# Cross-attention with layer norm: layer norm spread over two steps, scores of every fourth step from another buffer, and a context of ten 512-column matmuls ahead of them

## The chip, the cores and the metric

The kernel runs on one core of a Trainium2 chip. Its engines are TensorE (matmuls; PE in the profile, its weight loads PEld), VectorE (DVE), ScalarE (ACT), GpSimd (POOL) and SyncE (SP), which here only starts DMAs, in order. Engines meet through semaphores alone. The metric is the device time of one execution in microseconds; lower is better. Three runs before the change took 322.92 to 323.16 us, median 322.97.

## The reference

Eight batches of 256 queries (width 256) attend to 256 context rows (width 192), with eight heads of width 256. Then come the output projection, the residual and a layer norm. Cut to what matters:

```
Q = (x @ Wq)  K = (ctx @ Wk)  V = (ctx @ Wv)          # 8 heads of 256
score = einsum('bhqd,bhkd->bhqk', Q, K) / 16           # masked where mask == 0
attn  = softmax(score, axis=-1)
out   = concat_heads(attn @ V) @ Wo + x
out   = (out - mean(out)) * rsqrt(var(out) + 1e-5) * gamma + beta
```

## The kernel before, in words

The weights are folded once: A = Wk Wq per head, so that scores are ctx (A x), and C = Wv Wo per head, so that the output is the sum over heads of (attn ctx) C. Every float32 operand is split into a hi part (rounded, by ScalarE) and a lo part (the rest, by VectorE or GpSimd), and each product is the sum of three matmuls, hi hi, hi lo and lo hi.

The work is a chain of 32 steps t = 4b + j: eight batches b, four pairs of heads j = 0 to 3. In step t TensorE does, in this order (`step`, L527 to L538): the scores of t (20 matmuls of 256 columns), the query products g of t + 1 (18), the output products of t - 4 (18), and the context products of t - 3 (20). So the context products of pair j = 0 stand at the end of a step with j = 3, and the scores of j = 0 follow right behind them. Steps 0 to 5 are written out, steps 6 to 29 are a loop over b = 1 to 6 whose body is j = 2, 3, 0, 1, and the end is written out again.

The scores' stationary operand is g: gU (the upper 64 rows of both heads, hi and lo together), gL_hi and gL_lo. For t < 5 (`EARLY`) `g_tiles` (L118) hands out another buffer, `g_early`, for the same three tiles; the moving operand is always ctxT_hi or ctxT_lo. TensorE waits for gU (g_split, L402) before the first score matmul, and for gL_lo (L411) before the fifth.

The other engines follow in each step. VectorE takes scores and mask to negated scores and the row maxima, ScalarE does the exponentials, VectorE the inverse of the sums, GpSimd the normalising of probs, VectorE a transpose in squares of 32 x 32 for each head (L829). Between the two transposes VectorE writes the lo parts of g for the next step (`gU_lo_part`, `gL_lo_part`). SyncE carries the squares to memory and back as pT_raw (`carry_squares`, L283): one DMA out (L286), a wait until it has landed (L289), four DMAs in (L294). The next step's first transpose on VectorE writes the same squares tile, and so waits until that DMA has landed (L825).

The layer norm of batch b - 1 is done in the steps of batch b. VectorE adds the residual and takes the statistics at the end of j = 3 (of batch b), GpSimd makes rstd, and VectorE centres y (L885) and normalises it (L892) in j = 0 of the next batch. SyncE's loop body (L304 to L312) is, in its order: load xT, ctxT and mask of the next batch, carry the squares of j = 1, 2 and 3, load ctx and x, carry the squares of j = 0, and store the output (`store_out`, L236, which waits for the second normalised tile). Behind the store, the next pass of the loop begins with the three loads and the squares of j = 1.

`context_products` (L430) writes into a whole bank; its helper `halves` (L439) splits each product into two matmuls of 256 columns, one for each head, and only for t = 0 uses one of 512.

Of the kernel before, what the change touches and what calls it, by code (L numbers as in the profile page):

```python
# [25 lines left out]
PAIRS = H // 2  # L26
# [13 lines left out]
EARLY = 5  # L40

def attention_kernel(nc, xT, x, ctxT, ctx, mask, wqT, wkT, wvT, wo, gamma, beta, out, scratch):
    es = ExitStack()
    with es:
# [70 lines left out]

        y_last = probs[0][:, 0:QT, :]

        def g_tiles(t):  # L118

            if isinstance(t, int) and t < EARLY:  # L120
                return tuple(g_early[:, n] for n in range(3))
            return gL_hi[:], gL_lo[:], gU[:]

# [3 lines left out]
        gL_bank = bank("gL_bank", [P, 2, S])  # L127
# [196 lines left out]
        def _(pe):  # L324
# [65 lines left out]

            def scores(t, j, b, heads=(0, 1)):

                L_hi, L_lo, U = g_tiles(t)

                if j == 0:

                    pe.wait_ge(ctxT_split, b + 1)
                for hh in heads:
                    if hh == 0:

                        pe.wait_ge(g_hi_done, 3 * t + 3)
                        pe.wait_ge(g_split, 3 * t + 2)  # L402
                    for q in range(QT):
                        rows = slice(q * P, (q + 1) * P)
                        hi, lo, up = L_hi[:, hh, rows], L_lo[:, hh, rows], U[:, hh, rows]
# [24 lines left out]
            def context_products(t, j, b):  # L430

                if j == 0:

                    pe.wait_ge(C_split, 2 * (PAIRS - 1))

                    pe.wait_ge(ctx_split, 2 * b + 2)
                hi, lo, tL, tU = pT_hi[j % 2], pT_lo[j % 2], places("tL", t)[0], places("tU", t)[0]

                def halves(into, stationary, moving, first=False, last=False):  # L439

                    if isinstance(t, int) and t == 0:

                        return split_products(into[:], [(stationary, moving)], first=first, last=last)
                    for hh in range(2):
                        ins = split_products(into[:, hh, :], [(stationary, moving[:, hh, :])],
                                             first=first and hh == 0, last=last, shared=True)
                    return ins

                pe.wait_ge(pT_hi_done, 2 * t + 2)
                if isinstance(t, int) and t == STEPS - 1:  # L450

                    for k in range(KT):
                        halves(tU, ctxU[:, k, :], hi[:, k], first=k == 0)
                    pe.wait_ge(pT_split, 2 * t + 2)
                    for k in range(KT):
                        upper = halves(tU, ctxU[:, k, :], lo[:, k], last=k == KT - 1)
                    upper.then_inc(t_product, 1)
                    for k in range(KT):
                        halves(tL, ctxL_hi[:, k, :], hi[:, k], first=k == 0)
                        halves(tL, ctxL_lo[:, k, :], hi[:, k])  # L460
                        lower = halves(tL, ctxL_hi[:, k, :], lo[:, k], last=k == KT - 1)
                    lower.then_inc(t_product, 1)
                    return
                for k in range(KT):
                    halves(tL, ctxL_hi[:, k, :], hi[:, k], first=k == 0)
                    halves(tL, ctxL_lo[:, k, :], hi[:, k])

                if isinstance(t, int) and STEPS - 4 <= t < STEPS - 2:

                    pe.wait_ge(tU_summed, 2 * t)  # L470
                for k in range(KT):
                    halves(tU, ctxU[:, k, :], hi[:, k], first=k == 0)
                by_squares = not (isinstance(t, int) and t >= STEPS - 2)
                for k in range(KT):

                    pe.wait_ge(pT_split, 2 * t + (k + 1 if by_squares else 2))
                    end = k == KT - 1
                    lower = halves(tL, ctxL_hi[:, k, :], lo[:, k], last=end)
                    if end:
                        lower.then_inc(t_product, 1)  # L480
                    upper = halves(tU, ctxU[:, k, :], lo[:, k], last=end)
                upper.then_inc(t_product, 1)
# [99 lines left out]
        def _(act):  # L582
            def hi_part(dst, src):
                return nc.scalar.activation(dst, src, ACT.Copy)  # L584
# [21 lines left out]
                act.wait_ge(ctxT_in, 16 * b + 16)  # L606
                hi_part(ctxT_hi[:], ctxT_raw[:]).then_inc(ctxT_hi_done, 1)

            def gU_hi_part(t):

                act.wait_ge(g_product, 2 * t + 1)
                U = g_tiles(t)[2]
                hi_part(U[0:UP, 0, :], gU_bank[0:UP, 0, :]).then_inc(g_hi_done, 1)
                hi_part(U[UP:P, 1, :], gU_bank[UP:P, 0, :]).then_inc(g_hi_done, 1)

            def gL_hi_part(t):

                act.wait_ge(g_product, 2 * t + 2)
                hi_part(g_tiles(t)[0], gL_bank[:]).then_inc(g_hi_done, 1)

            def exponentials(t, j, heads=(0, 1)):
                if not (isinstance(t, int) and t < 2):
# [60 lines left out]
            def step(t, j, b, folds=()):  # L683
                before = not (isinstance(t, int) and t < OUT_LAG)
                if before:
                    t_hi_part(t - OUT_LAG)
                if j == PAIRS - 1 and not (isinstance(t, int) and t < PAIRS):
                    ctx_hi_part(b)
                exponentials(t, j, heads=[0])
                if before:  # L690
                    tU_hi_part(t - OUT_LAG)
                exponentials(t, j, heads=[1])
                if j == PAIRS - 1:
                    ctxT_hi_part(b + 1)
                gU_hi_part(t + 1)
                gL_hi_part(t + 1)
                if j == 2 and not (isinstance(b, int) and b == B - 1):
                    xT_hi_part(b + 1)
                if isinstance(t, int) and t == 1:
                    ctx_hi_part(b)  # L700
                if not (isinstance(t, int) and t < LAG - 1):
                    pT_hi_part(t - LAG + 1, (j - LAG + 1) % PAIRS)
                for pair in folds:
                    C_hi_part(pair)
# [6 lines left out]
            xT_hi_part(0)  # L711
            for h in range(2, H - 2):
                A_hi_part(h)
            gU_hi_part(0)
            gL_hi_part(0)
            ctxT_hi_part(0)
            for h in range(H - 2, H):
                A_hi_part(h)
# [29 lines left out]
        def _(dve):  # L748
# [33 lines left out]
                dve.wait_ge(mask_lowered, b + 1)  # L782
                nc.vector.tensor_scalar(mask_bias[:], mask_low[:], 4.0, None, ALU.mult).then_inc(mask_ready, 1)

            def gU_lo_part(t, hh):

                dve.wait_ge(g_hi_done, 3 * t + 1 + hh)
                own, other = (slice(0, UP), slice(UP, P))[::1 if hh == 0 else -1]
                U = g_tiles(t)[2]
                lo_part(U[other, hh, :], gU_bank[own, 0, :], U[own, hh, :]).then_inc(g_split, 1)  # L790

            def gL_lo_part(t):

                dve.wait_ge(g_hi_done, 3 * t + 3)
                L_hi, L_lo, _ = g_tiles(t)
                lo_part(L_lo, gL_bank[:], L_hi).then_inc(g_split, 1)

            def maxima(t, b, heads=(0, 1)):
# [97 lines left out]
            def centre(b):  # L896
                for q in range(QT):
                    if q == 0:

                        dve.wait_ge(mean_done, QT * b + QT)  # L900
                    centre_tile(y, q)
# [7 lines left out]
            def step(t, j, b, ends=None, folds=()):  # L909
# [16 lines left out]
                    finish_mask(b + 1)  # L926
                if by_squares:
                    transpose_squares(t, j, 0)
                if ends is not None and j == 0:
                    centre(ends)  # L930
                gU_lo_part(t + 1, 0)
                gU_lo_part(t + 1, 1)
                gL_lo_part(t + 1)
                if by_squares:
                    transpose_squares(t, j, 1)
                if ends is not None and j == 0:
                    normalise(ends)
                if ends is not None and j == 3:
                    add_residual(ends)
# [4 lines left out]
            dve.sem_inc(out_bank_read, 1)  # L944
            for h in range(H - 2):
                A_lo_part(h)
            gU_lo_part(0, 0)
            gU_lo_part(0, 1)
            gL_lo_part(0)
            for h in range(H - 2, H):  # L950
                A_lo_part(h)
            lower_mask(0)
# [7 lines left out]
            with dve.Fori(1, B - 1) as b:  # L960
                step(PAIRS * b + 2, 2, b)
                step(PAIRS * b + 3, 3, b, ends=b - 1)
                step(PAIRS * b + 4, 0, b + 1, ends=b - 1)
                step(PAIRS * b + 5, 1, b + 1)
            step(STEPS - 2, 2, B - 1)

            t_lo_part_lower(STEPS - 5)
# [186 lines left out]
```

## Time and profile before

| | |
|---|---|
| median of three runs | 322.97 us |
| the profiled execution | 323.15 us |
| its span, first to last instruction | 321.3 us |
| TensorE busy | 314.5 us (98%), 2574 matmuls |
| VectorE, ScalarE, GpSimd busy | 253.1 (79%), 221.9 (69%), 181.1 (56%) us |

The page gives the engines' busy time and 40 slices of the span. As TensorE's matmuls overlap, its pace is read from the starts in the timeline and not from the length of one (0.28 us). In a timeline a row is start, duration, engine, line, operation, output and inputs, count, and in brackets the idle time before it with its releaser.

### The profile page before, as it was taken

The numbers are of one execution on the slowest core, as the hardware profiler recorded it, in microseconds if no ns is written. First come the engines' busy times: TensorE is split into PE (matmuls) and PEld (weight loads), VectorE is DVE, ScalarE is ACT, GpSimd is POOL, SyncE is SP. The second block draws the span as 40 slices with busy tenths as digits, with TensorE's granted clock in tenths as the row PEclk, the third lists the DMA queues.
The fourth block names the chain that finished last, engine by engine and source line by source line (L and its number), as shares of the span: only waits on it lengthen the run. The fifth ranks groups of instructions, "written<-read, shape, count | busy, mean of one in ns | idle before, by whom it ended". The sixth has DMA issues, their size and how long they took to land.

```text
span 321.3 us, 8037 instructions
## 1 busy us (share of the span) xinstructions
PE 314.5 (98%) x2574; PEld 308.1 (96%) x2574; DVE 253.1 (79%) x721; ACT 221.9 (69%) x601; POOL 181.1 (56%) x183
## 2 busy tenths in 40 slices
PE   8999999999999999999999999999999999999993
PEld 7998888999999999999999999999999999999992
DVE  0466878778998889977997799977997799975686
ACT  2446677678777797668767787768766887767640
POOL 1122476558855586548755686457845686447311
PEclk9999999999999999999999999999999999999999
DMA  7995453453444545364356435354257435440001
GB/s 255 369 406 204 135 166 130 139 197 133 135 128 161 191 150 165 132 201 149 114 186 198 149 94 187 125 205 155 104 170 207 168 82 171 162 134 0 35 0 65
DMA packets 46911, 50.27 MB, mean 156 GB/s; under 512 B 3504, under 2 KB 37040, under 8 KB 46896
## 3 DMA queue, kind: packets, MB, share of 16 engines
q1 hardware_dynamic: 46608, 49.56, 46.1%
q10 hardware_dynamic: 288, 0.52, 0.7%
q8 instruction: 8, 0.13, 0.2%
q14 instruction: 7, 0.06, 0.1%
HBM read 32.24 MB, written 17.83 MB: 156 GB/s over the span
## 4 chain that ended last, share of the span: by engine, by line
PE 95%; DMA 2%; DVE 1%; SPq 1%; POOLq 0%; issue 0%; POOL 0%
PE score_bank L328 24%; PE out_bank L328 19%; PE gL_bank L328 14%; PE tL_bank L328 14%; PE tU_bank L328 9%; PE gU_bank L328 7%; DMA wq_raw<-in_wqT 2%; PE spare_bank L328 1%; PE spare_bank L362 1%; PE tL_bank L362 1%; PE tL_bank L344 1%; PE tU_bank L344 1%; PE out_bank L368 1%; PE tU_bank L368 1%; PE out_bank L344 0%; PE spare_bank L344 0%
## 5 line engine op out<-in xcount | busy, mean ns | idle before, releaser
L1033 POOL TENSOR_TENSOR probs<-probs,inv_sum 128x512 f32<-128x512 f32 x64 | 66.6, 1041 | 88.1 <-DVE inv_sum L819 87.5
L628 ACT ACTIVATE probs<-neg_scores,neg_max 128x256 f32<-128x256 f32 x128 | 64.2, 502 | 32.7 <-DVE neg_max L808 32.7
L1056 POOL TENSOR_TENSOR pT_lo<-pT_raw,pT_hi 128x512 fp32r<-128x512 f32 x60 | 76.5, 1295 | 8.6 <-ACT pT_hi L584 8.6
L808 DVE CUSTOM_DVE_ANT_0 neg_scores<-score_bank,mask_bias 128x256 f32<-128x256 f32 x128 | 49.2, 421 | 6.2 <-PE score_bank L328 3.7
L584 ACT ACTIVATE tL_hi<-tL_bank 128x512 fp32r<-128x512 f32 x31 | 18.6, 599 | 38.0 <-PE tL_bank L328 38.0
L829 DVE STREAM_TRANSPOSE squares<-probs 128x512 f32<-128x512 f32 x60 | 42.3, 706 | 0.6 <-DMA scratch<-squares 0.4
L754 DVE TENSOR_TENSOR tL_lo<-tL_bank,tL_hi 128x512 fp32r<-128x512 f32 x31 | 21.4, 689 | 22.7 <-ACT tL_hi L584 22.6
L328 PE MATMUL gL_bank<-xT_hi,A_hi 128*128 128x256 f32 x128 | 35.6, 278 | 0.0
L328 PE MATMUL gL_bank<-xT_lo,A_hi 128*128 128x256 f32 x128 | 35.6, 278 | 0.0
L328 PE MATMUL gL_bank<-xT_hi,A_lo 128*128 128x256 f32 x128 | 35.6, 278 | 0.0
L584 ACT ACTIVATE pT_hi<-pT_raw 128x512 fp32r<-128x512 f32 x60 | 34.3, 623 | 0.0
L328 PE MATMUL out_bank<-CL_lo,tL_hi 128*128 128x256 f32 x118 | 32.9, 279 | 0.0
L328 PE MATMUL out_bank<-CL_hi,tL_hi 128*128 128x256 f32 x118 | 32.9, 279 | 0.0
L328 PE MATMUL out_bank<-CL_hi,tL_lo 128*128 128x256 f32 x118 | 32.9, 279 | 0.0
L328 PE MATMUL score_bank<-ctxT_hi,gL_lo 128*128 128x256 f32 x108 | 30.1, 279 | 0.0
L328 PE MATMUL score_bank<-ctxT_hi,gL_hi 128*128 128x256 f32 x108 | 30.1, 279 | 0.0
L328 PE MATMUL score_bank<-ctxT_lo,gL_hi 128*128 128x256 f32 x108 | 30.1, 279 | 0.0
L328 PE MATMUL score_bank<-ctxT_hi,gU 128*128 128x256 f32 x108 | 30.1, 279 | 0.0
L328 PE MATMUL score_bank<-ctxT_lo,gU 128*128 128x256 f32 x108 | 30.1, 279 | 0.0
L856 DVE TENSOR_TENSOR tU<-tU_bank,tU_moved 64x256 f32<-64x256 f32 x62 | 26.0, 419 | 1.6 <-ACT tU_moved L669 0.6
L328 PE MATMUL tL_bank<-pT_hi,ctxL_hi 128*128 128x256 f32 (+1 forms) x122 | 24.6, 282 | 0.0
L328 PE MATMUL tL_bank<-pT_hi,ctxL_lo 128*128 128x256 f32 (+1 forms) x122 | 24.5, 281 | 0.0
(176 smaller groups left out, 1007.2 us busy)
## 6 DMA issues: line engine op xcount, KB each, us to landing
scratch<-squares SPq DMA_DIRECT2D x30, 512.0 KB, 2.6
pT_raw<-scratch SPq DMA_DIRECT2D x120, 128.0 KB, 3.1
xT_raw<-in_xT SPq DMA_DIRECT2D x8, 256.0 KB, 3.6
ctxT_raw<-in_ctxT SPq DMA_DIRECT2D x8, 256.0 KB, 3.8
wo_raw<-in_wo SPq DMA_DIRECT2D x4, 512.0 KB, 13.6
x_res<-in_x SPq DMA_DIRECT2D x8, 256.0 KB, 3.2
out<-y SPq DMA_DIRECT2D x7, 256.0 KB, 2.5
wq_raw<-in_wqT SPq DMA_DIRECT2D x3, 512.0 KB, 7.8
```

The lines of the kernel that those rows point to most:

```text
L328: ins = nc.tensor.matmul(into, stationary, moving, start=first and n == 0, stop=last and n == len(pairs) - 1, skip_group_check=shared)
L344: ins = nc.tensor.matmul(dst[:, i * DL:(i + 1) * DL], wq_raw[:, h * DT + d, i * P:(i + 1) * P], wk_raw[:, h * DT + d, :], start=d == 0, st ...
L362: ins = nc.tensor.matmul(lower[:, hh, :], wv_raw[:, h * DT + d, 0:P], wo_raw[:, h * DT + d, :], start=d == 0, stop=d == DT - 1)
L368: ins = nc.tensor.matmul(upper[hh * UP:(hh + 1) * UP, 0, :], wv_raw[:, h * DT + d, P:DL], wo_raw[:, h * DT + d, :], start=d == 0, stop=d = ...
L584: return nc.scalar.activation(dst, src, ACT.Copy)
L628: nc.scalar.activation(probs[j % 2][:, n, :], neg_scores[:, n, :], ACT.Exp, bias=neg_max[:, n:n + 1], scale=-1.0, accum_out=row_sum[:, n:n ...
L754: return nc.vector.tensor_tensor(dst, whole, hi.bitcast(F32), ALU.subtract)
L808: nc.vector.tensor_tensor_reduce(out=neg_scores[:, n, :], in0=score_bank[hh][:, q, :], in1=mask_bias[:], scale=-SCALE, scalar=3.0e38, op0= ...
L829: nc.vector.transpose(squares[:, :, rows, :].rearrange("p s n c -> p n s c"), probs[j % 2][:, rows, :].rearrange("p n (s c) -> p n s c", c ...
L856: nc.vector.tensor_tensor(tU[part, :], places("tU", t)[0][part, hh, :], tU_moved[part, :], ALU.add).then_inc(tU_summed, 1)
L1033: nc.gpsimd.tensor_tensor(probs[j % 2][:, rows, :], probs[j % 2][:, rows, :], inv, ALU.mult) \
L1056: nc.gpsimd.tensor_tensor(pT_lo[j % 2][:, k].rearrange("p hh (q i r) -> p (hh q) i r", q=QT, i=ROWS), pT_raw[j % 2][:, k].rearrange("p i n ...
```

## The change

Four edits. `g_tiles` gets j as well, and hands out `g_early` in every step with j = 0, not only for t < 5. `halves` uses one matmul of 512 columns whenever its pair is j = 0. On VectorE the centring of y stays in steps j = 0, but moves from ahead of the lo parts of g to behind the second transpose; the normalising moves from there to the same place of the step j = 1. SyncE's, GpSimd's and ScalarE's orders stay (ScalarE writes g_early instead of gU and gL_hi in these steps).

```diff
-        def g_tiles(t):
+        def g_tiles(t, j):
-            if isinstance(t, int) and t < EARLY:
+            if j == 0 or isinstance(t, int) and t < EARLY:
                 return tuple(g_early[:, n] for n in range(3))
...
                 def halves(into, stationary, moving, first=False, last=False):
-                    if isinstance(t, int) and t == 0:
+                    if j == 0:
                         return split_products(into[:], [(stationary, moving)], first=first, last=last)
...
-                if ends is not None and j == 0:
-                    centre(ends)
-                gU_lo_part(t + 1, 0)
-                gU_lo_part(t + 1, 1)
-                gL_lo_part(t + 1)
+                gU_lo_part(t + 1, (j + 1) % PAIRS, 0)
+                gU_lo_part(t + 1, (j + 1) % PAIRS, 1)
+                gL_lo_part(t + 1, (j + 1) % PAIRS)
                 if by_squares:
                     transpose_squares(t, j, 1)
                 if ends is not None and j == 0:
+                    centre(ends)
+                if ends is not None and j == 1:
                     normalise(ends)
...
-                step(PAIRS * b + 5, 1, b + 1)
+                step(PAIRS * b + 5, 1, b + 1, ends=b - 1)
```

What stands on TensorE before, in the loop, at the end of a step (context products into tL_bank and tU_bank, then the next scores):

```order
L449 ISA
L328 MATMUL tL_bank<-pT_hi,ctxL_hi 128x256 x2
L328 MATMUL tL_bank<-pT_hi,ctxL_lo 128x256 x2
L328 MATMUL tL_bank<-pT_hi,ctxL_hi 128x256 x2
L328 MATMUL tL_bank<-pT_hi,ctxL_lo 128x256 x2
L328 MATMUL tU_bank<-pT_hi,ctxU 128x256 x4
L476 REGISTER_ALU
L328 MATMUL tL_bank<-pT_lo,ctxL_hi 128x256 x2
```

And now, at the end of the loop's step j = 3 and the start of j = 0:

```order
L328 MATMUL tU_bank<-pT_hi,ctxU 128x512 x2
L476 REGISTER_ALU
L328 MATMUL tL_bank<-pT_lo,ctxL_hi 128x512
L328 MATMUL tU_bank<-pT_lo,ctxU 128x512
L328 MATMUL tL_bank<-pT_lo,ctxL_hi 128x512
L328 MATMUL tU_bank<-pT_lo,ctxU 128x512
L401 ISA
L402 REGISTER_ALU
L328 MATMUL score_bank<-ctxT_hi,g_early 128x256
L328 MATMUL score_bank<-ctxT_lo,g_early 128x256
```

The pairs of 256 columns have become single matmuls of 512, and the scores behind them read g_early; the count of columns is the same.

On VectorE, before, the end of the loop's step j = 0 (L885 centres, L754 are the lo parts of g and then of tL, L829 the transposes, L892 normalises):

```order
L829 STREAM_TRANSPOSE squares<-probs 128x2x8x32
L885 SCALAR_TENSOR_TENSOR y<-y,mean_var,gamma_sb 128x256 x2
L787 ISA
L754 TENSOR_TENSOR gU<-gU_bank,gU 64x256
L787 REGISTER_ALU
L754 TENSOR_TENSOR gU<-gU_bank,gU 64x256
L794 REGISTER_ALU
L754 TENSOR_TENSOR gL_lo<-gL_bank,gL_hi 128x512
L829 STREAM_TRANSPOSE squares<-probs 128x2x8x32
L892 SCALAR_TENSOR_TENSOR y<-y,rstd,beta_sb 128x256 x2
L845 ISA
L754 TENSOR_TENSOR tL_lo<-tL_bank,tL_hi 128x512
```

Now the same place:

```order
L829 STREAM_TRANSPOSE squares<-probs 128x2x8x32
L787 ISA
L754 TENSOR_TENSOR gU<-gU_bank,gU 64x256
L787 REGISTER_ALU
L754 TENSOR_TENSOR gU<-gU_bank,gU 64x256
L794 REGISTER_ALU
L754 TENSOR_TENSOR gL_lo<-gL_bank,gL_hi 128x512
L829 STREAM_TRANSPOSE squares<-probs 128x2x8x32
L885 SCALAR_TENSOR_TENSOR y<-y,mean_var,gamma_sb 128x256 x2
L845 ISA
L754 TENSOR_TENSOR tL_lo<-tL_bank,tL_hi 128x512
```

And the end of the loop's step j = 1, which before had nothing between its second transpose and the loop's branch:

```order
L754 TENSOR_TENSOR gL_lo<-gL_bank,gL_hi 128x512
L829 STREAM_TRANSPOSE squares<-probs 128x2x8x32
L892 SCALAR_TENSOR_TENSOR y<-y,rstd,beta_sb 128x256 x2
L960 REGISTER_ALU
L960 COMPARE_AND_BRANCH
```

The centring no longer stands ahead of gU and gL_lo, and the normalising is one step later.

## Rows read from the trace of the kernel before

**Rows 1.** The page: busy us (share) xinstructions; granted TensorE clock in 40 slices.
```profile
PE 314.5 (98%) x2574; PEld 308.1 (96%) x2574; DVE 253.1 (79%) x721; ACT 221.9 (69%) x601; POOL 181.1 (56%) x183
...
PEclk9999999999999999999999999999999999999999
```
**Rows 2.** Timeline of PE: first score matmuls of steps 6, 7, 14, 15.
```profile
68.70 0.28 PE L328 MATMUL score_bank<-ctxT_hi,gU 128*128 128x256 f32 x1
...
77.31 0.28 PE L328 MATMUL score_bank<-ctxT_hi,gU 128*128 128x256 f32 x1
...
139.31 0.28 PE L328 MATMUL score_bank<-ctxT_hi,gU 128*128 128x256 f32 x1
...
148.26 0.28 PE L328 MATMUL score_bank<-ctxT_hi,gU 128*128 128x256 f32 x1
```
**Rows 3.** Timeline of PE, step 9, fourth to sixth score matmul.
```profile
94.88 0.28 PE L328 MATMUL score_bank<-ctxT_lo,gL_hi 128*128 128x256 f32 x1
95.00 0.30 PE L328 MATMUL score_bank<-ctxT_hi,gL_lo 128*128 128x256 f32 x1
95.14 0.28 PE L328 MATMUL score_bank<-ctxT_hi,gU 128*128 128x256 f32 x1
```
**Rows 4.** Timeline of DVE, end of step 8.
```profile
92.08 1.15 DVE L885 SCALAR_TENSOR_TENSOR y<-y,mean_var,gamma_sb 128x256 f32<-128x256 f32 x2
...
94.17 0.69 DVE L754 TENSOR_TENSOR gL_lo<-gL_bank,gL_hi 128x512 fp32r<-128x512 f32 x1
94.78 0.71 DVE L829 STREAM_TRANSPOSE squares<-probs 128x512 f32<-128x512 f32 x1
95.40 0.95 DVE L892 SCALAR_TENSOR_TENSOR y<-y,rstd,beta_sb 128x256 f32<-128x256 f32 x2
```
**Rows 5.** Timeline of PE: query products ahead of the first g_early scores and behind them.
```profile
15.28 0.28 PE L328 MATMUL gL_bank<-xT_hi,A_hi 128*128 128x256 f32 x1
...
16.58 0.28 PE L328 MATMUL gL_bank<-xT_hi,A_lo 128*128 128x256 f32 x1
...
22.59 0.28 PE L328 MATMUL gL_bank<-xT_hi,A_hi 128*128 128x256 f32 x1
...
23.83 0.28 PE L328 MATMUL gL_bank<-xT_hi,A_lo 128*128 128x256 f32 x1
```
**Rows 6.** Timeline of PE: context of t = 0 in 512 columns, scores of step 4.
```profile
50.43 0.39 PE L328 MATMUL tL_bank<-pT_lo,ctxL_hi 128*128 128x512 f32 x1
...
51.35 0.28 PE L328 MATMUL score_bank<-ctxT_hi,g_early 128*128 128x256 f32 x1
...
53.74 0.28 PE L328 MATMUL gU_bank<-xT_hi,A_hi 128*128 128x256 f32 x1
```
**Rows 7.** Timeline of the SP queue (DMA issues), step 13.
```profile
136.08 0.37 SPq L239 DMA_DIRECT2D out<-y  x1
137.09 0.35 SPq L221 DMA_DIRECT2D xT_raw<-in_xT  x1
...
138.61 0.33 SPq L286 DMA_DIRECT2D scratch<-squares  x1
```
**Rows 8.** Line L286, the squares' DMA issued at 104.78, 138.61, 174.38.
```profile
DMA to landing us min/median/max: 4.2/4.2/4.2
...
DMA to landing us min/median/max: 4.9/4.9/4.9
...
DMA to landing us min/median/max: 4.1/4.1/4.1
```
**Rows 9.** Timeline of DVE: transposes of steps 5 and 10, gL_lo behind the latter.
```profile
67.42 0.70 DVE L829 STREAM_TRANSPOSE squares<-probs 128x512 f32<-128x512 f32 x1
...
109.04 0.71 DVE L829 STREAM_TRANSPOSE squares<-probs 128x512 f32<-128x512 f32 x1 [0.39 <-DMA scratch<-squares]
...
110.69 0.69 DVE L754 TENSOR_TENSOR gL_lo<-gL_bank,gL_hi 128x512 fp32r<-128x512 f32 x1
```
**Rows 10.** The page, DMA issues: count, KB, median us to landing.
```profile
scratch<-squares SPq DMA_DIRECT2D x30, 512.0 KB, 2.6
```

More of the change, by code:

```diff
@@ L391, in scores @@
             def scores(t, j, b, heads=(0, 1)):
-                L_hi, L_lo, U = g_tiles(t)
+                L_hi, L_lo, U = g_tiles(t, j)
                 if j == 0:
@@ L607, in ctxT_hi_part, with gU_hi_part, gL_hi_part @@
                 hi_part(ctxT_hi[:], ctxT_raw[:]).then_inc(ctxT_hi_done, 1)
-            def gU_hi_part(t):
+            def gU_hi_part(t, j):
                 act.wait_ge(g_product, 2 * t + 1)
-                U = g_tiles(t)[2]
+                U = g_tiles(t, j)[2]
                 hi_part(U[0:UP, 0, :], gU_bank[0:UP, 0, :]).then_inc(g_hi_done, 1)
                 hi_part(U[UP:P, 1, :], gU_bank[UP:P, 0, :]).then_inc(g_hi_done, 1)
-            def gL_hi_part(t):
+            def gL_hi_part(t, j):
                 act.wait_ge(g_product, 2 * t + 2)
-                hi_part(g_tiles(t)[0], gL_bank[:]).then_inc(g_hi_done, 1)
+                hi_part(g_tiles(t, j)[0], gL_bank[:]).then_inc(g_hi_done, 1)
             def exponentials(t, j, heads=(0, 1)):
@@ L694, in step @@
                     ctxT_hi_part(b + 1)
-                gU_hi_part(t + 1)
-                gL_hi_part(t + 1)
+                gU_hi_part(t + 1, (j + 1) % PAIRS)
+                gL_hi_part(t + 1, (j + 1) % PAIRS)
                 if j == 2 and not (isinstance(b, int) and b == B - 1):
@@ L713, in _ @@
                 A_hi_part(h)
-            gU_hi_part(0)
-            gL_hi_part(0)
+            gU_hi_part(0, 0)
+            gL_hi_part(0, 0)
             ctxT_hi_part(0)
@@ L783, in finish_mask, with gU_lo_part, gL_lo_part @@
                 nc.vector.tensor_scalar(mask_bias[:], mask_low[:], 4.0, None, ALU.mult).then_inc(mask_ready, 1)
-            def gU_lo_part(t, hh):
+            def gU_lo_part(t, j, hh):
                 dve.wait_ge(g_hi_done, 3 * t + 1 + hh)
                 own, other = (slice(0, UP), slice(UP, P))[::1 if hh == 0 else -1]
-                U = g_tiles(t)[2]
+                U = g_tiles(t, j)[2]
                 lo_part(U[other, hh, :], gU_bank[own, 0, :], U[own, hh, :]).then_inc(g_split, 1)
-            def gL_lo_part(t):
+            def gL_lo_part(t, j):
                 dve.wait_ge(g_hi_done, 3 * t + 3)
-                L_hi, L_lo, _ = g_tiles(t)
+                L_hi, L_lo, _ = g_tiles(t, j)
                 lo_part(L_lo, gL_bank[:], L_hi).then_inc(g_split, 1)
@@ L946, in _ @@
                 A_lo_part(h)
-            gU_lo_part(0, 0)
-            gU_lo_part(0, 1)
-            gL_lo_part(0)
+            gU_lo_part(0, 0, 0)
+            gU_lo_part(0, 0, 1)
+            gL_lo_part(0, 0)
             for h in range(H - 2, H):
```

## The prediction

> **What bounds the kernel now.** I read the page's busy shares first, then the timeline of TensorE, then those of VectorE and of the SyncE queue around one batch boundary, and last the landings of the squares DMA. TensorE is busy for 314.5 of 321.3 us at a granted clock of full speed in every slice [rows 1], so 2.4 GHz throughout, and nothing is missing to fill: only fewer or faster matmuls, or a new wait, can move the end.
>
> The reader should look at the starts. A step has 76 matmuls of 256 columns (20 scores, 18 query products, 18 output, 20 context). Step 6 runs from 68.70 to 77.31, 8.61 us or 113.3 ns each; step 14 runs from 139.31 to 148.26, 8.95 us or 117.8 ns each [rows 2]. The instructions are the same, the clock is the same and TensorE shows no gap in either. So there are two paces, 4.5 ns apart, and each lasts until something disturbs it. All steps to 8 have the fast one; from step 9 to the last steps all have the slow one.
>
> The change of pace has a place. In step 9 the fifth score matmul, the first to read gL_lo, starts at 95.00 and its successor at 95.14 instead of 0.113 later [rows 3]. gL_lo of this step was written by VectorE from 94.17 for 0.69, to 94.86, and ahead of it and gU stands the centring of y, 1.15 us from 92.08 [rows 4]. Without the centring gL_lo would be there at 93.71. A wait of a few hundredths was enough, and the fast pace did not come back by itself.
>
> What brings it back? Query product 0 ran 11 intervals from 15.28 to 16.58, 118 ns each, slow. Then came the first scores with g_early. The query products behind them ran 11 intervals from 22.59 to 23.83, 113 ns each, fast [rows 5]. Step 4 is the only place that has what all steps j = 0 have after the change: a context in 512 columns, 0.92 us for four matmuls (230 ns), then 20 scores with g_early in 2.39 us (51.35 to 53.74, 119.5 ns each) [rows 6], and behind it the fast pace again.
>
> **The change part by part.** Write S(t) for the start of step t's scores.
>
> Scores with g_early at t = 8, 12, ... 28: six times 20 matmuls at 119.5 ns instead of 117.8 (at t = 8 instead of 113.3). +0.03 each, +0.12 at t = 8.
>
> Context in 512 columns at the end of t = 11, 15, ... 27 (and 7, 31): ten at 230 ns against twenty at 117.8: 2.30 against 2.36, -0.05 each; against twenty at 113.3 (2.27) +0.03.
> The Trainium skill has a price here ("TensorE: Matmul & The Clock Gate", section Back-to-back issue gap): columns over 2.4 GHz plus about 2.5 ns for a matmul by itself, so 215.8 ns for 512 columns. This trace shows 230 [rows 6]; by the page's figure ten would take 2.16 us and each context would give another 0.14 us, an estimate.
>
> Pace, if it comes back at every j = 0: the steps j = 0, 1, 2 run fast. j = 0 takes 2.39 + 56 x 0.1133 = 8.73 us instead of 8.95 (-0.22), j = 1 and 2 take 8.61 (-0.34 each).
>
> The centring moves behind gL_lo and behind the second transpose of the squares. Per batch VectorE does as much as before. In step 8 gL_lo is ready at 93.71, 1.1 us before it is asked for, so step 9 is not disturbed: t = 9 and 10 gain 0.34 each. The squares of j = 0 steps are there 1.15 us earlier too.
>
> The normalising moves from the end of j = 0 to the end of j = 1. Here a queue pays that the diff does not touch. SyncE waits for y_out_done before it stores the output, and behind that store stand, in its one queue, the loads of xT, ctxT and mask and the squares of the same step j = 1. Before, the store of batch 1 was issued at 136.08 and the squares at 138.61, 2.53 us later, all without a wait [rows 7]. Now the store waits for the end of the normalising. In an undisturbed step the second transpose starts at 67.42 [rows 9]; the normalising starts 0.62 later, as from 94.78 to 95.40, and takes 0.95 [rows 4], so it ends at 68.99, S(6) + 0.29. The squares' DMA then goes out at S + 0.29 + 2.53 = S + 2.82 of the next step (j = 2), where it stood at S(14) - 0.70. Behind those loads it landed 4.2, 4.9, 4.1, 4.1 and 4.9 us later (steps 9, 13, 17, 21, 25; rows 8 show the first three) [rows 8], so at S + 6.9 to 7.7, and at 4.2 at S + 7.02.
>
> Who waits for it: VectorE's first transpose of step j = 2 (in step 10 it would have started at 109.04 - 0.39 = 108.65), and behind it gU, gL_lo and so TensorE's next scores. In step 10 this wait already shows: transpose at 109.04, 0.39 idle, gL_lo finished at 110.69 + 0.69 = 111.38, 2.34 after the transpose's start [rows 9]. With 0.06 from landing to transpose and 0.14 from gL_lo to its matmul [rows 3, 4], the fifth score matmul of the step j = 3 can start at S + 7.02 + 2.54 = S + 9.56. At the fast pace it is due at S + 8.61 + 0.45 = S + 9.06. So TensorE waits 0.50 us (0.40 at a landing of 4.1, 1.20 at 4.9). It happens after steps 10, 14, 18, 22 and 26; after the last store no loads follow, and step 30 transposes on TensorE. I take 4.2, the median of the five landings. That wait also costs the fast pace, as it did in step 9, so j = 3 stays at 117.8 ns until the next g_early scores.
>
> Sum against the profiled run's own span of 321.3: t = 8, +0.12; t = 9 and 10, -0.68; five groups of four steps (11 to 14, ..., 27 to 30), each -0.05 - 0.22 - 0.34 - 0.34 = -0.95, together -4.75; five waits of 0.50, +2.50; t = 31 and what follows to the transposes on TensorE, 58 matmuls x 4.5 ns, -0.26. Together -3.07. The profiled run took 323.15; the median of the runs, 322.97, is 0.18 below it. Forecast: 322.97 - 3.0 = 320.0 us, with own ends of 319.4 (all landings 4.1) and 323.4 (all landings 4.9).
>
> **Rivals.**
> 1. No wait at all. If the squares land 3.7 us or less after their issue (2.6 is the median of all 30 [rows 10]), gL_lo is in time, nothing disturbs the fast pace, and j = 3 gains too (56 x 0.1133 + 2.30 = 8.65, -0.30 instead of -0.05). Sum: 0.12 - 0.68 - 5 x 1.20 - 0.25 = -6.8, so 316.2 us. For it: the four reads of pT before the store are now over by the time of the loads. Against it: step 10 before, where the landing behind the three loads decided.
> 2. The pace does not come back in the loop. All five examples of g_early scores stand in code that runs once, and none was entered from the slow pace of 256-column matmuls. Then t = 9 and 10 gain 0.68, t = 8 costs 0.12, and the first wait makes the rest slow. At the slow pace the normalising ends at S + 0.1 and the wait is 0 to 0.7 a batch; with two of five landings at 4.9, +1.4. Sum +0.8, so 323.8 us. The page just named, same section, knows a gap that depends on columns alone and no lasting pace; by it the near weights would change nothing and this is the outcome. The two step lengths [rows 2] speak against the page: equal work, 0.34 us apart.
> 3. Slower through the queue. The pace comes back, but the loads and the squares, bunched behind the late store, land later than they did. The gains are 5.56 us in all, 1.11 for each of the five waits; from a landing of 4.8 us the waits eat them. At 5.3 us each wait is 1.60 and the sum is 5 x 1.60 - 5.56 = +2.4, so 325.4 us. For it: two landings of five at 4.9 already. Against it: this window then holds less traffic, not more.
> A smaller doubt lies inside all of these: the fast pace has not been seen across the loop's back edge (between j = 1 and 2). If it were lost there, six steps j = 2 would cost 0.34 each, 2.0 us more, less what the wait shrinks by.
>
> **How the numbers follow.** Forecast 0.48, rival 1 0.20, rival 2 0.17, rival 3 0.15. A measurement of this kernel tells 0.2%, 0.65 us, from no change: faster is below 322.3, slower above 323.6. Faster: 0.42 of the forecast, rival 1 whole, 0.03 of rival 3, 0.65. Same: 0.05 of the forecast, 0.06 of rival 2, 0.03 of rival 3, 0.14. Slower: the rest, 0.21. The range runs from just under rival 1 to rival 2's 323.8; below and above it lies less than 0.2.
>
> **What will show it.** Right, if the trace after has: score matmuls 113.3 ns apart in steps 9 and 10; after each j = 0 steps of 8.6 us; the output store issued some 0.3 us after the start of j = 2 instead of in the middle of j = 1; the first transpose of j = 2 waiting for the DMA of the squares; and a gap on TensorE before the first or fifth score matmul of each j = 3. Wrong, if steps after the first j = 0 stay at 8.95 us (rival 2), if j = 3 is fast as well (rival 1), or if the gap is over 1.1 us (rival 3).

## The result and the profile after

| | before | after |
|---|---|---|
| median | 323.07 us (4 runs, 322.92 to 323.20) | 328.20 us (4 runs, 326.96 to 328.55) |
| ratio, 95% interval | | 1.0152 [1.0123, 1.0181] |
| profiled execution / its span | 323.15 / 321.3 us | 327.89 / 326.1 us |

The change makes the kernel 1.5% slower. The forecast was 320.0 us with a range of 315.8 to 323.8, so it missed, and on the wrong side.

The page after, busy shares and the chain that ended last by engine; then the row of the view of waits on TensorE (us in total, times, longest):

```profile
PE 314.5 (96%) x2504; PEld 303.0 (93%) x2504; DVE 261.7 (80%) x721; ACT 221.9 (68%) x601; POOL 183.6 (56%) x183
...
PE 58%; DVE 14%; issue 10%; DMA 8%; ACT 4%; SPq 3%; DVEq 1%; ACTq 0%; POOLq 0%; POOL 0%
```
```profile
PE score_bank L328 <- DVE gU L754: 4.8, 5, 1.5
```

TensorE is busy for as long as in [rows 1], in a span 4.8 us longer, and the chain of work that ended last, which before was TensorE's for 95% of the span, now runs over the other engines and the DMAs for 42% of it. Five waits have appeared, all on gU of the steps j = 3. They are the ones that the forecast saw, but not of its size. (The view counts the gap ahead of the first score matmul; the forecast and the text below reckon to the fifth, the first that reads gL_lo.) The chain of waits of the changed kernel ahead of the first one (start, duration, what):

```profile
103.23 1.82 DVE y L892 x2
105.20 0.38 SPq L239
...
106.28 0.35 SPq L221
106.73 0.38 SPq L224
107.29 0.33 SPq L234
...
107.79 4.06 DMA scratch<-squares
111.88 0.08 DVE squares L829
...
113.07 0.44 DVE gU L754
113.55 2.52 PE score_bank L328 x17
```

The reader should see the whole mechanism in order: the normalising (L892), then in SyncE's queue the store (L239), the loads of xT, ctxT and mask, then the squares' DMA, 4.06 us, the transpose, gU, and last the scores of step 11. The same place in the timelines of VectorE, SyncE and TensorE (start, duration, engine, line, operation, idle before it in brackets):

```profile
94.25 1.88 DVE L885 SCALAR_TENSOR_TENSOR y<-y,mean_var,gamma_sb 128x256 f32<-128x256 f32 x2
96.06 0.68 DVE L754 TENSOR_TENSOR tL_lo<-tL_bank,tL_hi 128x512 fp32r<-128x512 f32 x1
...
103.15 1.88 DVE L892 SCALAR_TENSOR_TENSOR y<-y,rstd,beta_sb 128x256 f32<-128x256 f32 x2
...
110.64 0.29 DVE L777 TENSOR_SCALAR mask_low<-mask_raw 128x256 f32<-128x256 int32 x1 [1.94 <-DMA mask_raw<-in_mask]
...
111.88 0.71 DVE L829 STREAM_TRANSPOSE squares<-probs 128x512 f32<-128x512 f32 x1 [0.87 <-DMA scratch<-squares]
```
```profile
105.20 0.38 SPq L239 DMA_DIRECT2D out<-y  x1
...
107.79 0.33 SPq L286 DMA_DIRECT2D scratch<-squares  x1
```
```profile
103.22 0.28 PE L328 MATMUL score_bank<-ctxT_hi,gU 128*128 128x256 f32 x1
...
113.55 0.38 PE L328 MATMUL score_bank<-ctxT_hi,gU 128*128 128x256 f32 x1 [1.55 <-DVE gU L754]
...
114.27 0.39 PE L328 MATMUL score_bank<-ctxT_hi,gL_lo 128*128 128x256 f32 x1
```

The centring, 1.15 us in [rows 4], and the normalising, 0.95 there, take 1.88 us each. VectorE waited for the mask as well (1.94 us, to 110.64), but the squares landed later, at 111.85, and set the transpose. The fifth score matmul of step 11 was due at 103.22 + 9.06 = 112.28 and starts at 114.27: a wait of 1.99 us where 0.50 was forecast.

The lengths of steps, each from the first score matmul of one step to that of the next in the timeline of TensorE, in us, of every kernel profiled (a wait ahead of scores counts to the step before). The names are those of the experiments below. A row is one run, and for e4 it is the odd one of five, 319.29 us:

```
step              8     9     10     11    12    13    14    15    16
before           8.61  8.96   8.96  8.95  8.95  8.95  8.95  8.95  8.95
after            8.74  8.61  10.33  9.26  8.99  8.95  9.51  9.25  8.72
e1 store late    8.74  8.61   8.61  8.64  8.74  8.61  8.74  8.89  8.74
e2 norm in j=0   8.74  9.21   8.95  8.90  8.99  8.95  8.95  8.90  8.72
e3 LN only       8.61  8.62  10.40  8.99  8.61  8.62 10.21  8.99  8.62
e4 weights only  8.74  8.61   9.48  9.25  9.00  8.95  8.95  8.89  8.73
e5 late, plain   8.61  8.61   8.84  8.96  8.95  8.95  8.95  8.95  8.95
e9 near only     8.74  8.62   8.61  8.61  8.75  8.61  8.62  8.61  8.74
e10 512 only     8.95  8.95   8.95  8.90  8.95  8.95  8.95  8.89  8.95
e11 weights late 8.74  8.61   8.61  8.64  8.74  8.61  8.61  8.64  8.74
e12 apart        8.74  8.62   8.78  9.01  8.74  8.61  8.62  9.20  8.73
e14 plain apart  8.61  8.62   8.61  8.61  8.62  8.61  8.61  8.62  8.61
e15 all near     8.75  8.75   8.74  8.75  8.75  8.74  8.75  8.75  8.74
e16 near, late   8.74  8.62   8.61  8.61  8.75  8.61  8.62  8.61  8.75
```

8.61 is the fast pace and 8.95 the slow one; 8.74 is a fast step with g_early scores.

### The profile page after: what moved, and what is told of

Read it like the earlier page. It is cut to its first block, busy times and chain, and to the rows that moved or that the text cites. A ratio compares the mean times of both kernels' runs of the same rounds, so it can differ in the third digit from the quotient of the medians.

```text
span 326.1 us, 7897 instructions
## 1 busy us (share of the span) xinstructions
PE 314.5 (96%) x2504; PEld 303.0 (93%) x2504; DVE 261.7 (80%) x721; ACT 221.9 (68%) x601; POOL 183.6 (56%) x183
## 4 chain that ended last, share of the span: by engine, by line
PE 58%; DVE 14%; issue 10%; DMA 8%; ACT 4%; SPq 3%; DVEq 1%; ACTq 0%; POOLq 0%; POOL 0%
PE score_bank L328 17%; PE out_bank L328 10%; PE gL_bank L328 8%; PE tL_bank L328 7%; DMA scratch<-squares 6%; PE tU_bank L328 5%; PE gU_bank L328 4%; ACT probs L628 4%; DVE y L892 3%; DVE gU L754 3%; DVE squares L829 2%; DMA wq_raw<-in_wqT 2%; DVE y L885 2%; DVE gL_lo L754 2%; PE spare_bank L328 1%
## 5 line engine op out<-in xcount | busy, mean ns | idle before, releaser
L1056 POOL TENSOR_TENSOR pT_lo<-pT_raw,pT_hi 128x512 fp32r<-128x512 f32 x60 | 79.6, 1347 | 8.6 <-ACT pT_hi L584 8.6
L829 DVE STREAM_TRANSPOSE squares<-probs 128x512 f32<-128x512 f32 x60 | 42.3, 706 | 4.6 <-DMA scratch<-squares 4.4
L328 PE MATMUL score_bank<-ctxT_hi,g_early 128*128 128x256 f32 x132 | 28.6, 286 | 0.0
L328 PE MATMUL score_bank<-ctxT_hi,gU 128*128 128x256 f32 x84 | 23.9, 284 | 4.8 <-DVE gU L754 4.8
L754 DVE TENSOR_TENSOR tL_lo<-tL_bank,tL_hi 128x512 fp32r<-128x512 f32 x31 | 21.1, 680 | 8.4 <-ACT tL_hi L584 8.4
L328 PEld LDWEIGHTS score_bank<-ctxT_hi,g_early 128*128 128x128 f32 x132 | 22.8, 190 | 1.7 <-issue 1.2
L328 PE MATMUL tL_bank<-pT_lo,ctxL_hi 128*128 128x256 f32 (+1 forms) x108 | 24.3, 294 | 0.0
L328 PE MATMUL tU_bank<-pT_lo,ctxU 128*128 128x256 f32 (+1 forms) x108 | 24.2, 295 | 0.0
```

The costliest lines, as they stand in the source:

```text
L328: ins = nc.tensor.matmul(into, stationary, moving, start=first and n == 0, stop=last and n == len(pairs) - 1, skip_group_check=shared)
L754: return nc.vector.tensor_tensor(dst, whole, hi.bitcast(F32), ALU.subtract)
L829: nc.vector.transpose(squares[:, :, rows, :].rearrange("p s n c -> p n s c"), probs[j % 2][:, rows, :].rearrange("p n (s c) -> p n s c", c ...
L1056: nc.gpsimd.tensor_tensor(pT_lo[j % 2][:, k].rearrange("p hh (q i r) -> p (hh q) i r", q=QT, i=ROWS), pT_raw[j % 2][:, k].rearrange("p i n ...
```

## The experiments

Times are medians. The kernel before took 323.06 us beside e1, e3, e4 and e5 (13 runs) and 323.10 beside e2, e14, e15 and e16 (15 runs). Beside e9 to e12 it ran 7 times, six times 322.91 to 323.50 and once 315.19; with that one among them a ratio would mislead, so the medians of these four stand against 323.15, that of the seven.

**e1, the store behind the squares of j = 1.** SyncE's loop was turned, so that the loads and the squares of j = 1 stand at the end of its body and the store behind them (the first and last passes are written out; cut):

```diff
-            with sp.Fori(1, B - 1) as b:
-                load_ahead(b + 1)
-                carry_squares(PAIRS * b + 1, 1)
+            load_ahead(2)
+            carry_squares(PAIRS + 1, 1)
+            with sp.Fori(1, B - 2) as b:
...
                 load_residual(b)
                 carry_squares(PAIRS * b + 4, 0)
+                load_ahead(b + 2)
+                carry_squares(PAIRS * b + 5, 1)
                 store_out(b - 1)
```

> The changed kernel with SyncE's queue in another order: the output's store stands behind the squares of step j = 1 instead of ahead of the loads and of these squares. Queue theory (the late store holds up the loads of xT, ctxT and mask and the squares, and through them TensorE): no wait on TensorE ahead of steps j = 3, the pace is never disturbed, all steps from 9 on take 8.6 to 8.75 us, about 316 us (range 315.5 to 317.5). Rival (VectorE itself is too late, since centring and normalising now take 1.88 us each beside GpSimd's work instead of 1.15 and 0.95): TensorE still waits about 1 us ahead of each j = 3, 321 to 323 us.

Measured: 317.40 us (316.99 to 318.16), ratio to before 0.9832 [0.9815, 0.9848]. No wait on TensorE is left ahead of steps j = 3. So the late store at the head of SyncE's queue is what made the changed kernel slow: 10.8 us lie between the two, by nothing but the place of one DMA in the order. VectorE's longer y operations (1.88 us here too) do not hold TensorE up by 1 us when the squares' DMA does not stand behind them; that rival falls. In step 14 the pace was lost once and came back in 16: VectorE's tU_lo ended at 143.58, and the weight load behind it started at 143.63, 0.02 us after its turn.

**e3, the layer norm's move alone.** Against the changed kernel:

```diff
-            if j == 0 or isinstance(t, int) and t < EARLY:
+            if isinstance(t, int) and t < EARLY:
...
-                    if j == 0:
+                    if isinstance(t, int) and t == 0:
```

> The layer norm's move alone: g_early only for t < 5 and contexts of 256 columns as before the change. Queue theory: the waits on TensorE stay (2.0 us ahead of step 11, about 1 us each at the slow pace ahead of 15, 19, 23, 27), and the pace never comes back after step 10: 8.95 us a step. Sum 323.1 - 0.7 + 2.0 + 4 x 1.0 = 328.4 us. If the near weights or the 512 columns were what costs time, this one is about as fast as before, 322 to 324 us.

Measured: 329.99 us (327.85 to 331.09), ratio 1.0202 [1.0156, 1.0248]. The waits, five again:

```profile
PE score_bank L328 <- DVE gU L754: 6.0, 5, 1.7
```

As expected, this part alone is the loss. One thing was not expected: in steps 12 and 13 the pace is fast without near weights (g_early only for t < 5), behind a wait of 1.4 us. A wait can take the fast pace away and can also give it back.

**e4, the weights' part alone.** Near weights and 512 columns, the layer norm where it was. Against the changed kernel:

```diff
+                if ends is not None and j == 0:
+                    centre(ends)
                 gU_lo_part(t + 1, (j + 1) % PAIRS, 0)
...
                 if ends is not None and j == 0:
-                    centre(ends)
-                if ends is not None and j == 1:
                     normalise(ends)
...
-                step(PAIRS * b + 5, 1, b + 1, ends=b - 1)
+                step(PAIRS * b + 5, 1, b + 1)
```

> The weights' part alone: g_early and 512-column contexts in all j = 0, the layer norm where it was. If g_early scores bring the fast pace back: j = 0 steps take 8.7 us, the centring disturbs again at the start of every j = 1, the rest stays at 8.95, so about 5 x 0.2 us less, 322 us. If they bring it back only some of the time (in the changed kernel in two batches of five): 322.5 us. If they never do in the loop: 323.3 us.

Measured: 316.51 us (five runs, 316.14 to 319.29), ratio 0.9797 [0.978, 0.9813]. All three expectations were too high. The centring does not disturb step 9 at all here, though it stands where it stood; the next kernel shows why. The profiled run is the odd one: VectorE waited 1.87 us for a mask load in step 10 and then for the squares, TensorE 0.70 us ahead of step 11, and the pace came back only in step 16. The other four runs took 316.14 to 316.64 us.

**e9, near weights alone**, contexts of 256 columns and the layer norm as before; **e10, 512 columns alone**. Each is e4 with one more line set back, e9 the first and e10 the second of these:

```diff
-                    if j == 0:
+                    if isinstance(t, int) and t == 0:
...
-            if j == 0 or isinstance(t, int) and t < EARLY:
+            if isinstance(t, int) and t < EARLY:
```

> The weights' part without the 512 columns: g_early in all j = 0, contexts of 256 columns, layer norm as before the change. If the g_early scores alone do it (they restore the pace, and their 0.12 us keeps the centring harmless): 316 to 317 us as with both. If the 512 columns ahead are needed: 322 to 323.5 us.

> 512-column contexts of j = 0 alone: g_early only for t < 5, layer norm as before the change. If the near weights are needed, the pace goes at step 9 as before and stays away: 322.5 to 323.3 us. If the 512 columns restore it by themselves in each j = 3: steps of j = 0 are fast again, 319 to 321 us.

Measured: e9 316.18 us (316.10 to 316.53), e10 323.10 us (321.87 to 323.23). The whole gain is in the near weights; the 512 columns do nothing alone and take 0.03 us in a step that is fast (8.64 in steps j = 3 of e1 against 8.61 or 8.62 in e9), as the sum had it. VectorE of e9 at the start of step 9, and TensorE's weight loads (PEld) there:

```profile
94.04 0.69 DVE L754 TENSOR_TENSOR gL_lo<-gL_bank,gL_hi 128x512 fp32r<-128x512 f32 x1
```
```profile
94.78 0.19 PEld L328 LDWEIGHTS score_bank<-ctxT_lo,gL_hi 128*128 128x128 f32 x1
94.89 0.19 PEld L328 LDWEIGHTS score_bank<-ctxT_hi,gL_lo 128*128 128x128 f32 x1
```

The same two weight loads of the kernel before:

```profile
94.77 0.19 PEld L328 LDWEIGHTS score_bank<-ctxT_lo,gL_hi 128*128 128x128 f32 x1
94.91 0.19 PEld L328 LDWEIGHTS score_bank<-ctxT_hi,gL_lo 128*128 128x128 f32 x1
```

In e9 gL_lo is there at 94.73 and its weight load follows the one before by 0.11 us, as all do. Before, gL_lo came at 94.86 [rows 4] and the load at 94.91, 0.14 behind the one ahead of it and so 0.03 late. It is the weight load that waits, and the matmul of 95.00 [rows 3] hardly shows it. The 20 scores from g_early made step 8 longer by 0.13 us, and VectorE's work did not become longer with it. So a cost on TensorE of 0.13 us in the step with the layer norm gave the centring the room that it lacked, and the 23 steps from 9 on kept their fast pace. The moved layer norm was not needed for that.

**e5, late store and moved layer norm without near weights and 512 columns:** the edits of e1 and of e3 together.

> Layer norm moved and the store late, but g_early only for t < 5 and contexts of 256 columns as before. If the fast pace simply lasts until something disturbs it, it lasts from step 5 to the last steps here with no help of near weights: all steps 8.61 us, 315.5 us (0.12 us less for each j = 0 step than with g_early). If the loop's back edge or anything else disturbs it once, all later steps take 8.95 us: up to 322.5 us.

Measured: 322.57 us (321.56 to 322.89), ratio 0.9981 [0.9971, 0.9991]. The pace was fast until it went in the middle of step 10, for the rest of the run. Where it went, in the timelines of VectorE, TensorE's weight loads and its matmuls (lines of the kernels with the late store are 8 higher: L900 is the normalising):

```profile
103.07 1.89 DVE L900 SCALAR_TENSOR_TENSOR y<-y,rstd,beta_sb 128x256 f32<-128x256 f32 x2
...
108.00 0.63 DVE L762 TENSOR_TENSOR tU_lo<-tU,tU_hi 128x256 fp32r<-128x256 f32 x1
```
```profile
108.46 0.19 PEld L336 LDWEIGHTS out_bank<-CL_hi,tL_lo 128*128 128x128 f32 x1
108.68 0.19 PEld L336 LDWEIGHTS out_bank<-CU_hi,tU_hi 128*128 128x128 f32 x1
```
```profile
108.69 0.39 PE L336 MATMUL out_bank<-CU_hi,tU_hi 128*128 128x256 f32 x1
108.91 0.28 PE L336 MATMUL out_bank<-CU_lo,tU_hi 128*128 128x256 f32 x1
```

tU_lo ends at 108.63, and the weight load that waits for it starts at 108.68 instead of 108.57, 0.11 us late. The matmul itself is only 0.01 late and the view of waits on TensorE's matmuls shows nothing, yet the next matmul comes 0.22 us later, and those that follow are 118 ns apart. tU_lo was late because the normalising had taken 1.89 us; e14 below, which adds only a wait on GpSimd that brings the normalising back to its short time, bears it out.

**e12, GpSimd held apart from the y operations.** The changed kernel with its own SyncE order; ahead of GpSimd's pT_lo in steps j = 0 and 1:

```diff
+                if behind is not None:
+                    pool.wait_ge(y_scaled_done if j == 0 else y_out_done, QT * behind + QT)
```

> The changed kernel, SyncE's order as in it, but GpSimd begins its pT_lo of steps j = 0 and j = 1 only when VectorE is through with the centring and the normalising. Port theory (two of the y operations take 1.88 us instead of 0.95 to 1.15 because GpSimd's pT_lo runs beside them, and this is 1.5 of the 2.0 us wait): both take 0.95 again, the store goes out 1.6 us earlier, the wait on TensorE falls from 2.0 to about 0.5 us where the pace is fast, and the time is 320 to 322 us, the forecast's own sum. Rival (the bunched loads are what makes the squares late): no change, 327 to 328.5 us.

Measured: 320.97 us (319.18 to 322.00) against 328.20. VectorE, GpSimd, SyncE and TensorE at the same place:

```profile
102.44 0.84 DVE L892 SCALAR_TENSOR_TENSOR y<-y,rstd,beta_sb 128x256 f32<-128x256 f32 x2
...
110.17 0.71 DVE L829 STREAM_TRANSPOSE squares<-probs 128x512 f32<-128x512 f32 x1 [0.88 <-DMA scratch<-squares]
```
```profile
103.36 2.55 POOL L1056 TENSOR_TENSOR pT_lo<-pT_raw,pT_hi 128x512 fp32r<-128x512 f32 x2 [2.69 <-DVE y L892]
```
```profile
106.04 0.33 SPq L286 DMA_DIRECT2D scratch<-squares  x1
```
```profile
112.57 0.39 PE L328 MATMUL score_bank<-ctxT_hi,gL_lo 128*128 128x256 f32 x1
```

With GpSimd out of the way the normalising takes 0.84 us. The squares go out 2.97 us after the start of step 10, against 4.57 in the changed kernel and 2.82 in the forecast, and the fifth score matmul of step 11 starts 0.44 us after its time (103.07 + 9.06 = 112.13). The five waits of this run, reckoned so, are 0.44, 0.24, 0.32, 0.15 and 0.53. They are together 1.68 us, about the forecast's wait of 0.50 each or less, and 320.97 is nearly its time (the profiled run is the fastest of four); the premise that failed was the length of the y operations.

**e14, all of it without near weights:** late store, moved layer norm and GpSimd held apart, g_early only for t < 5, 256 columns: the edits of e1, e3 and e12 together, or e5 with that of e12.

> The late store and the moved layer norm without near weights and without 512 columns, as the second late-store kernel (322.57 us), plus GpSimd's pT_lo held back until the centring and the normalising are done. In that kernel the fast pace went in step 10, where tU_lo came at 108.63 for a matmul due at 108.68, because the normalising had taken 1.89 us. If the fast pace lasts until something comes late, it now lasts from step 5 to the end, across the loop's back edges and without near weights: 315.3 us. If near weights or something else is needed to keep it: 321 to 323 us.

Measured: 315.40 us (315.22 to 315.47), ratio 0.9763 [0.9748, 0.9778]: the fastest of all, with every step from 5 on at 8.61 or 8.62, across the loop's back edges. tU_lo of step 10 now ends 1.0 us before its matmul:

```profile
107.14 0.63 DVE L762 TENSOR_TENSOR tU_lo<-tU,tU_hi 128x256 fp32r<-128x256 f32 x1
```
```profile
108.77 0.28 PE L336 MATMUL out_bank<-CU_hi,tU_hi 128*128 128x256 f32 x1
```

So the fast pace, once there, needs no near weights; it needs that no operand comes late. And the one run of the kernel before that took 315.19 us fits: where the margin is a few hundredths, the centring can also come in time, for a whole run. (That run has no profile, so this is inferred.)

**e15, g_early in every step,** layer norm and contexts as in e9:

```diff
-            if j == 0 or isinstance(t, int) and t < EARLY:
+            if True:
```

> g_early in every step, layer norm and contexts as before the change. If scores from g_early always take 119.5 to 120 ns and the matmuls behind them 113.3: all steps 8.74 us, 316.8 us (22 steps 0.21 us less than before, and half a us in the end). If what restores the pace is the change from one buffer to the other and not the buffer: 322 us or more.

Measured: 318.88 us (318.79 to 319.28), ratio 0.9876 [0.9861, 0.9891]. The steps are what was expected, 8.74 or 8.75 in all; the sum in the expectation was wrong (27 steps, 5 to 31, of 0.13 us more than 8.61, on top of e14's 315.4, make 318.9). The buffer, and not the change of buffers, makes its own scores 120 ns apart, and the fast pace of what follows is kept. It does not make that pace: in the changed kernel the same scores at step 12 are followed by matmuls 118 ns apart (8.99 us, and 8.95 for step 13).

**e2, the normalising back behind the centring in j = 0.**

```diff
                 if ends is not None and j == 0:
                     centre(ends)
-                if ends is not None and j == 1:
                     normalise(ends)
...
-                step(PAIRS * b + 5, 1, b + 1, ends=b - 1)
+                step(PAIRS * b + 5, 1, b + 1)
```

> The changed kernel with the normalising back in j = 0, right behind the centring. The store is early again, so no wait for the squares ahead of j = 3. But VectorE begins step j = 1 about 2.8 us of y work late (1.88 beside GpSimd and 0.95), so tU_lo is 0.5 us late for the upper output products of j = 1: TensorE waits 0.5 us in each of six such steps and the pace may go there until the next j = 0. 319.5 us if the pace stays, 325 us if it always goes; the rival, that the store's place alone decided, says 316.5 us.

Measured: 322.56 us (ten runs, 322.05 to 323.08), ratio 0.9983 [0.9974, 0.9992]. VectorE at the end of step 8, and TensorE where it waits in step 9:

```profile
94.26 1.88 DVE L885 SCALAR_TENSOR_TENSOR y<-y,mean_var,gamma_sb 128x256 f32<-128x256 f32 x2
96.06 0.87 DVE L892 SCALAR_TENSOR_TENSOR y<-y,rstd,beta_sb 128x256 f32<-128x256 f32 x2
...
99.98 0.62 DVE L754 TENSOR_TENSOR tU_lo<-tU,tU_hi 128x256 fp32r<-128x256 f32 x1
```
```profile
100.17 0.28 PE L328 MATMUL out_bank<-CL_hi,tL_lo 128*128 128x256 f32 x1
100.66 0.39 PE L328 MATMUL out_bank<-CU_hi,tU_hi 128*128 128x256 f32 x1 [0.21 <-DVE tU_lo L754]
```

The squares are never late now, and the time is 5.6 us below the changed kernel's. Beside GpSimd's pT_lo the centring takes 1.88, in the gap behind it the normalising takes 0.87. Their 2.7 us in a row (94.26 to 96.93) make tU_lo late for step 9 by 0.4 us, and the pace goes there. It comes back in steps 16 and 24 only, which puts the time between the expectation's two ends. TensorE's view of waits has this gap once and not six times. In step 17, behind a fast 16, the weight load behind tU_lo starts 0.21 us late (171.95 for 171.74) and the pace goes again, with no wait in that view; in step 13, at the slow pace, tU_lo ends 0.34 us ahead of its weight load (136.11 and 136.45).

**e11 and e16, the weights' part with the late store,** with and without 512 columns: e4 and e9 with the edit of e1.

> The weights' part alone with the store behind the squares of j = 1. In the profiled run of the weights' part alone (319.29 us) TensorE waited 0.7 us ahead of step 11, for a mask load 1.9 us late and the squares behind it; its other runs took 316.1 to 316.6. If the store ahead of the loads had a part in that, this version shows no such run and takes 316.2 us in all; else it is the same in the median (316.5) and may show one.

> The kernel before with g_early in all j = 0 and the store behind the squares of j = 1, nothing else: layer norm as before, contexts of 256 columns. Both parts by themselves gave 316.2 us; together no less is to be had while TensorE never waits: 316.1 us, and no run above 316.6.

Measured: e11 316.27 us (316.11 to 316.44), e16 316.28 us (316.15 to 316.52), the latter's ratio 0.9792 [0.9779, 0.9805]. Neither showed a run like e4's of 319.29, but nine runs are few to say that the late store is the reason, and e9, without it, showed none in four either; in the median moving the store is worth nothing where it is not late to begin with.

## Why the prediction was wrong, by its own steps

**The two paces: right.** Steps 9 and 10 are fast as soon as gL_lo is not late, e14 holds the fast pace to the end, and equal code runs at 8.61 or 8.95 us a step. The doubt about the loop's back edge was empty. What makes the two paces was not predicted and is not shown.

**What lost the pace in step 9: right,** to a few hundredths: gL_lo's weight load was 0.03 us late, and 0.13 us more room (e9) was enough. One reading is off: by its own rows gL_lo at 93.71 would be 1.3 us ahead of its matmul at 95.00, and not 1.1; nothing hangs on it. The prediction did not draw the conclusion. It had the near weights at +0.12 us for step 8 as a pure cost, and it took the centring to need a move.

**The wait through SyncE's queue: the mechanism right, the size wrong.** This is the step that failed: "the normalising starts 0.62 later, as from 94.78 to 95.40, and takes 0.95". That length was read where GpSimd's pT_lo was about to end, at 95.67; GpSimd's row of before:

```profile
93.12 2.55 POOL L1056 TENSOR_TENSOR pT_lo<-pT_raw,pT_hi 128x512 fp32r<-128x512 f32 x2 [0.57 <-ACT pT_hi L584]
```

In the new place pT_lo runs beside nearly all of it. The two tiles of y and the two of pT_lo in the changed kernel (duration in ns min/median/max, first and last start):

```profile
L892 DVE SCALAR_TENSOR_TENSOR y<-y,rstd,beta_sb x2: 444/984/1525, 103.1 to 103.5; 128x256 f32<-128x256 f32 x2
```
```profile
L1056 POOL TENSOR_TENSOR pT_lo<-pT_raw,pT_hi x2: 1302/1428/1555, 101.9 to 103.2; 128x512 fp32r<-128x512 f32 x2
```

The tiles of y took 0.444 and 1.525 us: the first slipped in at 103.15 ahead of the second pT_lo, and the second, from 103.5, ended only at 105.03, behind it.

The trace of before had a sign of it. The first tile of the centring took 0.751 us there and the second 0.475, with GpSimd's normalising of probs running beside the first until 92.55:

```profile
L885 DVE SCALAR_TENSOR_TENSOR y<-y,mean_var,gamma_sb x1: 751/751/751, 92.1 to 92.1; 128x256 f32<-128x256 f32 x1
```
```profile
91.51 1.04 POOL L1033 TENSOR_TENSOR probs<-probs,inv_sum 128x512 f32<-128x512 f32 x1 [0.80 <-DVE inv_sum L819]
```

The times of 1.88 us are +0.93 for the normalising and +0.73 for the centring, which pushes all of VectorE's step j = 1, less the 0.14 that step 9 could absorb: 1.52 us. Another 0.23 the forecast had at nothing or too small: the store went out 0.17 after the normalising's end, and the squares 2.59 after the store instead of 2.53. So the squares went out at S(10) + 4.57 instead of + 2.82. Their landings (4.1, 4.2, 4.0, 4.3 and 4.1 us, against 4.2 in the forecast) and the 2.39 us from the transpose's start to the matmul, against 2.48, were nearly as reckoned. The five waits at the fifth score matmul were 1.99, 0.81, 1.58, 0.93 and 1.63, together 6.94 us instead of 2.50: 4.4 us of the miss. e12 takes the overlap away and measures 0.44.

The Trainium skill states a lock that fits ("SBUF — State Buffer", section Who interferes with whom): a VectorE instruction with two SBUF inputs contends with a GpSimd instruction that reads SBUF, and whoever comes second waits for the other's whole instruction. By that rule the trace agrees: the second tile of y waited for the second pT_lo, which itself took 1.555 us instead of 1.302, and gL_lo, with one input in PSUM, kept its 0.69 us beside the first. The prediction did not weigh it.

**The pace at each j = 0: wrong.** It came back in steps 16 and 24, but not in 12, 20 and 28 (8.99 and then 8.95 a step). The forecast had five examples of five, all entered from other code. Three batches without it are 3 x (0.26 + 0.34 + 0.34) = 2.8 us, and 0.26 in the end: 3.1 of the miss. With the 4.4 of the waits that is 7.5 of the 7.9 us between the forecast change of the span, -3.1, and the measured +4.8; 0.4 is not accounted for. e2 shows the same three misses in the same steps, and e12, with shorter waits, had none in these steps. Why g_early scores bring the pace back from one entry and not from another stays open.

**The small terms** (g_early +0.12, 512 columns +0.03 in a fast step) were right.

**Rivals.** Rival 3, the slower one through the queue, is what happened; it had a chance of 0.15 and named the right place and price, but its cause, bunched loads, was not it: no landing was above 4.3 us, where two of before were 4.9. Its 1.11 us per wait as the point from which it decides was passed on average (1.39). Rival 2 held for three batches of five. Rival 1, no wait at all, did not happen here; e1, which takes the waits away by another order, is near its 316.2 us, at 317.4.

## What to carry to other kernels

When an instruction is moved, its duration has to be read again for the new neighbours: look at what GpSimd does in that stretch, and at the operation's longest time, not its median. Ask of every wait in a DMA queue what stands behind it; here one store, late by nothing but the time of its input, stood ahead of work that others wait for, and putting it behind that work took 10.8 us off. Where TensorE has no gaps and still two step lengths, look for the place at which the length changes, and there at the starts of the weight loads: the pace went at weight loads 0.02 to 0.21 us late, which TensorE's view of waits did not show.

## What the runs showed that was not expected

TensorE at a full granted clock, 2.4 GHz, has more than one steady distance between the same matmuls of 256 columns: 113.3 ns or 117.8, and 120 for scores from g_early. The first two each last for tens of microseconds. A weight load that started late by 0.02 us (e1, step 14), 0.21 us (e2, step 17), 0.03 us (before, step 9) or 0.11 us (e5) went with the turn from the fast to the slow one, in the last two for the remaining 190 to 200 us, and a wait of over 1 us with the turn back (e3), though not every such wait. The 4.5 ns between the two cost 2.4% of the whole kernel (e14 against before). What sets the distance, and what property of g_early makes it 120 ns, stays open.
